# A two-layer decoder on one core: expert output products turned to features, the recurrence reordered, unread matmuls added

## The reference, cut to what matters

```python
# layer 0 experts: top 2 of 8, and a shared expert
y   = einsum('eth,ehd->etd', silu(xf @ w1[e]) * (xf @ w3[e]), w2[e])
out = einsum('etd,te->td', y, cw) + (silu(xf @ sw1) * (xf @ sw3)) @ sw2
# layer 1 recurrence
xi, z = split(x @ Win.T); lam = exp(-8 * softplus(omega) * sigmoid(xi @ Wl.T + bl)); v = xi @ Wv.T + bv
h = lam_t * (h - 2 * v_t * (v_t.h / v_t.v_t)) + (1 - lam_t) * xi_t     # over t, from h = xi_0
out = (silu(z) * h) @ Wout.T
# layer 1 experts
y = selu(x @ exp_wi[e] + bi) @ exp_wo[e] + bo, weighted by the top 2 of 8 of a gate network
```

## Time and profile before

| | us |
|---|---|
| median of 3 runs | 1028.47 |
| lowest, highest | 1027.62, 1028.54 |
| the profiled execution | 1027.66 |
| its span, first to last instruction | 1025.9 |
| PE busy | 890.1 (87%) |
| PE weight loads busy | 659.5 (64%) |
| DVE busy | 807.4 (79%) |
| ACT busy | 544.1 (53%) |
| POOL busy | 421.4 (41%) |

### The profile page before, as it was taken

The page is one execution under the profiler, slowest core; times in us unless marked ns, Lnnn a source line. Parts: engine busy times, 40 slices in busy tenths (PEclk is TensorE's granted clock), DMA queues, the critical chain, the costliest instruction groups (busy, mean ns, idle before and its releaser), DMA issues.

```text
span 1025.9 us, 15128 instructions
## 1 busy us (share of the span) xinstructions
PE 890.1 (87%) x5606; PEld 659.5 (64%) x5606; DVE 807.4 (79%) x1443; ACT 544.1 (53%) x980; POOL 421.4 (41%) x401
## 2 busy tenths in 40 slices
PE   5967777777989999998985875899999899999997
PEld 4422323232769888885653554576667799899997
DVE  6699999999776555563888787679997788788886
ACT  6456565655553222235652221556658757667774
POOL 6479999999310010110885244544431111011110
PEclk9979999999999999998986998879999999999999
DMA  6000000000000100100000000100000000000001
GB/s 189 1 0 1 0 1 1 0 1 1 1 1 17 32 16 16 32 1 0 1 1 0 1 1 1 41 2 3 2 2 2 1 22 21 22 1 22 26 16 42
DMA packets 19859, 13.80 MB, mean 13 GB/s; under 512 B 3067, under 2 KB 18313, under 8 KB 19786
## 3 DMA queue, kind: packets, MB, share of 16 engines
q1 hardware_dynamic: 19786, 12.84, 4.5%
HBM read 11.79 MB, written 1.05 MB: 13 GB/s over the span
## 4 chain that ended last, share of the span: by engine, by line
PE 55%; DVE 16%; ACT 5%; issue 4%; POOL 2%; DVEq 0%; ACTq 0%; POOLq 0%
PE ps L1416 19%; PE ps L1409 18%; PE ps L1629 3%; PE ps L1460 2%; PE ps L1749 2%; DVE small L1259 2%; POOL R L370 2%; DVE G L1262 1%; PE ps L1739 1%; PE ps L1699 1%; DVE R L1220 1%; DVE stats L838 1%; DVE ps L1225 1%; PE ps L1816 1%; DVE ps L1209 1%
## 5 line engine op out<-in xcount | busy, mean ns | idle before, releaser
L1416 PE MATMUL ps<-xhl,whl 128*128 128x512 f32 x960 | 245.8, 405 | 6.6 <-ACT G L655 1.9
L1416 PEld LDWEIGHTS ps<-xhl,whl 128*128 128x128 f32 x960 | 177.7, 192 | 45.2 <-issue 7.7
L1409 PEld LDWEIGHTS ps<-R,G 128*128 128x128 f32 x1024 | 120.6, 194 | 7.0 <-DVE G L1303 4.8
L1409 PE MATMUL ps<-R,G 128*128 128x128 f32 x1024 | 121.3, 277 | 4.1 <-DVE G L1303 4.1
L793 ACT ACTIVATE G<-ps,w_exp_bi 128x512 f32<-128x512 f32 x128 | 89.9, 702 | 63.5 <-PE ps L1416 52.5
L361 POOL TENSOR_TENSOR R<-G,R 128x1024 f32<-128x1024 f32 x43 | 100.5, 2353 | 19.7 <-ACT R L556 17.1
L655 ACT ACTIVATE G<-ps 128x512 f32<-128x512 f32 x72 | 42.8, 597 | 114.4 <-PE ps L1416 114.4
L968 DVE TENSOR_TENSOR_SCAN R<-ps,R 128x1024 f32<-128x1024 f32 x43 | 97.5, 2277 | 5.7 <-POOL R L370 5.7
L794 ACT ACTIVATE G<-ps,ebs 128x512 f32<-128x512 f32 x144 | 102.0, 708 | 0.0
L1065 DVE SCALAR_TENSOR_TENSOR X<-ps,cw,X 128x128 f32<-128x128 f32 x272 | 76.5, 343 | 23.4 <-PE ps L1409 23.2
L1439 PE MATMUL ps<-bc,sel 96*128 96x512 bf16 x128 | 46.4, 390 | 50.2 <-ACT LN L563 22.2
(11 more groups left out here) (276 smaller groups left out, 1721.0 us busy)
## 6 DMA issues: line engine op xcount, KB each, us to landing
ew<-in_w_dram SPq DMA_DIRECT2D x24, 128.0 KB, 2.2
R<-in_exp_wi_dram SPq DMA_DIRECT2D x8, 256.0 KB, 2.8
R<-in_exp_wo_dram SPq DMA_DIRECT2D x8, 256.0 KB, 3.2
X<-in_x_dram SPq DMA_DIRECT2D x4, 256.0 KB, 4.1
out_dram<-X SPq DMA_DIRECT2D x4, 256.0 KB, 2.3
w_ctxT<-in_ctxT_dram SPq DMA_DIRECT2D x1, 487.5 KB
ew<-in_sw_dram SPq DMA_DIRECT2D x3, 128.0 KB, 2.6
w_W_in<-in_W_in_dram SPq DMA_DIRECT2D x1, 256.0 KB, 3.1
```

The lines of the kernel that those rows point to most:

```text
L1409: ins = mm(bank(o)[:, 0, b * width:(b + 1) * width], lhs(k, b), rhs(k), start=k == 0, stop=k == ks - 1)
L1416: ins = mm(mix(out) if n == N_WIN1 else out, whl[:, wslot(n), i, m * P:(m + 1) * P], rhs, start=k == 0, stop=k == 2)
```

## The change: what it does

Most of the diff renames semaphores. What is left:

1. First experts: chunks 0 to 3 (shared expert) and 8 to 31 (experts 1 to 6) make their output product with the weights as the stationary operand, both operands split, 6 matmuls of 512 columns; the result has features on partitions. ACT copies the hidden chunk to an upper part, DVE subtracts for the lower one, GpSimd splits the output weights. The router's weights are turned by PE, written to DRAM by SP and read back spread over all partitions, one expert at a time. DVE multiplies and adds into `YT`; at the end PE turns it and DVE adds it to X. Chunks 4 to 7 and 32 to 35 stay as they were.
2. Recurrence: values before decays; sigmoid becomes tanh, 0.5 (1 + tanh(x/2)), with its constants in `coef`; xz(1) to xz(3) stand in group 0 after the spread; chunk_dots(g - 1) stand ahead of v_dot_v(g); squares are summed into 64 columns instead of one.
3. `unread(o, n)`: n fp32 matmuls of 128 columns, identity times identity, into a bank that nobody reads, at the places shown.
4. Second experts: selu of chunk 1 ahead of the ranking, of chunk 2 in it; output banks 4 to 7 for the first four chunks.

```diff
+            def hidden_upper(i):                                   # ACT
+                if i >= 2:
+                    act.wait_ge(S["down0"], i - 1)
+                for m in range(M0):
+                    act.wait_ge(S["hid0"], M0 * i + m + 1)
+                    sc.copy(hl[:, i % 2, 0, m * GT:(m + 1) * GT], hidr[:, i % 2, m * GT:(m + 1) * GT])
...
+            def hidden_lower(i):                                   # DVE
+                for m in range(M0):
+                    dve.wait_ge(S["hid_hi"], M0 * nth(i) + m + 1)
+                    v.tensor_tensor(hl[:, i % 2, 1, ...], hidr[:, i % 2, ...], hl[:, i % 2, 0, ...], ALU.subtract)
+            def weigh_out(c):
+                e, g = divmod(c, NG)
+                dve.wait_ge(S["down0"], c + 1)
+                dve.wait_ge(S["cw_odd" if e % 2 else "cw_even"], 16 * (e // 2))
+                v.tensor_tensor(yt_new[:, c % 2], bank(4 + c % 2)[:, 0, :], cwb[:, e % 2, gcols(g)], ALU.mult)
+            def add_out_T(c):
+                v.tensor_tensor(YT[:, gcols(g)], YT[:, gcols(g)], yt_new[:, c % 2], ALU.add)
...
             for i in range((E + 1) * NG + 1):
+                if i - 2 in by_feature[NG:]:
+                    weigh_out(i - 2)
                 if i < (E + 1) * NG:
-                    hidden(i)
+                    hidden(i, (lambda: add_out_T(i - 2)) if i - 2 in by_feature[NG:] else (lambda: None))
+                if i in by_feature:
+                    hidden_lower(i)
...
+                if k == 2:                                         # SP
+                    sp.wait_ge(S["cw_rows"], 1)
+                    sp.dma_start(cw_dram.rearrange("e (b t) -> b e t", t=T), cw_rows)
+                    sp.wait_ge(S["cw_rows"], 17)
+                if k and k * NG in by_feature:
+                    sp.dma_start(cwb[:, k % 2, :], cw_dram[k - 1].partition_broadcast(P))
...
+            def down_T(c):                                         # PE
+                for k in range(M0):
+                    pe.wait_ge(S["hid_lo"], M0 * n + k + 1)
+                    for p, (i, j) in enumerate(PARTS):
+                        ins = mm(bank(4 + c % 2)[:, 0, :], w2hl[:, e % 2, i, k * D:(k + 1) * D],
+                                 hl[:, c % 2, j, k * GT:(k + 1) * GT], start=k == p == 0, stop=k == M0 - 1 and p == 2)
...
-            for g in range(NG - 1):
-                transpose_xn(3, g)
+            transpose_xn(3, 0)
+            transpose_xn(3, 1)
+            pe.wait_ge(S["yt_res"], NG)
+            unread(7, 5)
+            transpose_xn(3, 2, between=3)
+            unread(7, 7)
...
             xz(0)
             transpose_xn(3, NG - 1)
-            xz(1)
             for g in range(NG):
                 pe.wait_ge(S["xz_ev"], 4 * g + HI)
-                lam_or_v(g, w["Wl"], (0, 1), "l_mm", (("v2_ev", HI * g), ("l_ev", HI * g)))
-                lam_or_v(g, w["Wv"], (2, 0), "v2_mm", (("v2_ev", HI * g - 1), ("l_ev", HI * g + 1)))
-                if g + 2 < NG:
-                    xz(g + 2)
+                lam_or_v(g, w["Wv"], (0, 1), "v2_mm", (("l_ev", HI * g), ("v2_ev", HI * g)))
+                lam_or_v(g, w["Wl"], (2, 0), "l_mm", (("l_ev", HI * g - 1), ("v2_ev", HI * g + 1)))
+                if g:
+                    chunk_dots(g - 1)
                 v_dot_v(g)
                 spread_reciprocal(g)
-                if g:
-                    chunk_dots(g - 1)
+                if g == 0:
+                    xz(1)
+                    xz(2)
+                    xz(3)
             chunk_dots(NG - 1)
...
+            pe.wait_ge(S["u_done"], 3 * (NG - 1))                  # ahead of the chunk loop
+            pe.wait_ge(S["c_done"], 2 * (NG - 1))
+            pe.wait_ge(S["e_ev"], NG - 1)
+            unread(5, 14)
...
+            unread(5, 34)                                          # behind the chunk loop
...
+                if g + 1 < NG:                                     # behind the values of groups 0 to 2
+                    pe.wait_ge(S["ln_xnT"], 4 * NG + 1)
+                    unread(0, 6)
...
+            unread(7, 8)                                           # ahead of the head loop
...
             selu_sum(0, 0, "act1", "hid1")
             gate_logits(3)
+            selu_sum(1, 1, "act1", "hid1")
             step(gate_top(3))
...
-            selu_sum(1, 1, "act1", "hid1")
+            dve.wait_ge(S["down1"], 1)
+            selu_sum(2, 0, "act1", "hid1")
```

More of the change, by code:

```diff
@@ L45 @@
 EB = 8
+VW = 64
 def decoder_program(nc, a, out):
@@ L194, in decoder_program @@
         cwT = G[0:E, 5, 1, :].rearrange("p (b t) -> p b t", b=B)
+        by_feature = [*range(NG), *range(2 * NG, E * NG)]
+        nth = by_feature.index
+        cwb = G[:, 0, :, :]
+        yt_new = G[:, 2, 0, 0:2 * GT].rearrange("p (s n) -> p s n", s=2)
+        cw_rows = G[:, 2, 0, 2 * GT:2 * GT + T]
+        YT = G[:, 2, 1, :]
+        cw_dram = nc.dram_tensor("cw_by_expert", (E, N), F32).ap()
         xi, z1, lam, vv, nb, ww = (GBUF(i) for i in range(6))
@@ L342, in _ @@
                                       pattern=[[-1, 32], [0, P]], channel_multiplier=1))
-            gp.memset(cw0[:], 1.0)
             step(gp.memset(hmask[:], 1.0))
@@ L686, in _ @@
             copy_xnT(3, NG - 1)
-            xz_copy(1)
             for g in range(NG):
                 for m in range(HI):
-                    act.wait_ge(S["l_mm"], HI * g + m + 1)
-                    sc.activation(row(lam[:, m], g), mix(bank(m)[:, 0, :]), ACT.Sigmoid, bias=w["bl"][:, m:m + 1])\
-                        .then_inc(S["l_ev"], 1)
-                for m in range(HI):
                     act.wait_ge(S["v2_mm"], HI * g + m + 1)
-                    sc.activation(row(vv[:, m], g), mix(bank(2 - 2 * m)[:, 0, :]), ACT.Identity, bias=w["bv"][:, m:m + 1])\
+                    sc.activation(row(vv[:, m], g), mix(bank(m)[:, 0, :]), ACT.Identity, bias=w["bv"][:, m:m + 1])\
                         .then_inc(S["v2_ev"], 1)
@@ L701, in _ @@
                 for m in range(HI):
+                    act.wait_ge(S["l_mm"], HI * g + m + 1)
+                    sc.activation(row(lam[:, m], g), mix(bank(2 - 2 * m)[:, 0, :]), ACT.Tanh, bias=coef[:, 0, m:m + 1], scale=0.5)\
+                        .then_inc(S["l_ev"], 1)
+                for m in range(HI):
                     act.wait_ge(S["l_ev"], HI * g + m + 1)
-                    sc.activation(row(lam[:, m], g), row(lam[:, m], g), ACT.Exp, scale=coef[:, 2, m:m + 1])\
+                    sc.activation(row(lam[:, m], g), row(lam[:, m], g), ACT.Exp, bias=coef[:, 2, m:m + 1], scale=coef[:, 2, m:m + 1])\
                         .then_inc(S["lam_done"], 1)
-                if g + 2 < NG:
-                    xz_copy(g + 2)
+                if g == 0:
+                    xz_copy(1)
+                    xz_copy(2)
+                    xz_copy(3)
                 if g >= 1:
@@ L1396, in _, with unread, transpose_xn @@
             mm = nc.tensor.matmul
-            def transpose_xn(i, g):
+            def unread(o, n):
+                for _ in range(n):
+                    mm(bank(o)[:, 0, 0:P], ident[:], ident[:], start=True, stop=True)
+            def transpose_xn(i, g, between=0):
                 for b in range(GB):
+                    if b == GB // 2:
+                        unread(7, between)
                     if b % (GB // 2) == 0:
@@ L1419, in _ @@
             pe.wait_ge(S["const"], 1)
+            unread(7, 18)
             transpose_xn(0, 0)
+            unread(7, 5)
             for g in range(NG):
@@ L1424, in _ @@
                     transpose_xn(0, g + 1)
+                if g == 0:
+                    unread(7, 3)
                 pe.wait_ge(S["w_split"], 1)
@@ L1576, in router_logits, with transpose_YT @@
                 ins.then_inc(S["rt_mm"], 1)
+            def down_T(c):
+                e, n = c // NG, nth(c)
+                pe.wait_ge(S["w2_split"], n // NG + 1)
+                if c >= 2:
+                    pe.wait_ge(S["res0"], c - 1)
+                for k in range(M0):
[3 more added lines that the diff above has]
+                                 hl[:, c % 2, j, k * GT:(k + 1) * GT], start=k == p == 0, stop=k == M0 - 1 and p == 2)
+                ins.then_inc(S["down0"], 1)
+            def transpose_YT(g):
+                pe.wait_ge(S["yt_acc"], (E - 3) * NG + g + 1)
+                if g >= 2:
+                    pe.wait_ge(S["yt_res"], g - 1)
+                for b in range(GB):
+                    ins = nc.tensor.transpose(bank(6 + g % 2)[:, 0, b * D:(b + 1) * D], YT[:, (g * GB + b) * T:(g * GB + b + 1) * T], ident[:])
+                ins.then_inc(S["yt_mm"], 1)
             for i in range((E + 1) * NG + 1):
```

165 lines of the change are left out of this document (117 added, 48 removed).

## The result

The changed kernel ran in 1024.21 us (median of 20 runs, 1020.17 to 1033.13), the kernel before in 1028.88 beside it (20 runs, 1026.59 to 1035.64). The ratio is 0.9948, with a 95% interval from 0.9927 to 0.9969: 5.4 us faster by the ratio, 4.7 by the medians. 1025.3 was predicted, so the time came out close. The gain did not: 2.8 us were forecast, and the kernel before had a median 0.4 us higher here than in the runs that the forecast started from. The stages show that the total is a sum of opposite terms, some of which hang on TensorE's clock and differ from one execution to the next.

A forecast was written before the change was run, and what follows sets the result against it. PE was taken to bound both expert stages, DVE's work per group the recurrence, with DVE and PE alternating in chunk loop and heads. Terms -7.5 + 16 - 1.2 - 1.8 - 0.8 - 4 - 3.5 = -2.8 gave 1025.3 us, range 1017 to 1036.

The forecast's parts named there:

- First experts, -7.5 predicted: First experts: output product by features in 28 chunks gains 11.5 us, added costs leave -7.5 (-9 to 0).
- turned result: First experts: turning the result back takes 16 transposes, 4 x 0.58, +2.3 us.
- the tail: End of first experts: DVE has last feature chunks, additions of the turned result and norm together, +1.0 us.
- Rival 3: First experts: DVE becomes the bound, six instructions at 0.75, the -7.5 becomes 0, time 1033 us; chance 0.12.
- The sentence of the Trainium skill: First experts, DVE: next instruction waits until the pipe has emptied; about 1 us of gain would go, not in the sum.
- Recurrence, +16 predicted: Layer 1 recurrence: dots ahead of squares leave DVE waiting 8.2 us per group, twice; +16 us (+11.5 to +23).
- Rival 1: Recurrence, groups 2 and 3: whole exposed stretch runs at 1.2 GHz, 11.7 instead of 8.2 us each, 1032; chance 0.20.
- rival 2: Recurrence: clock survives the wait, 5.9 us exposed each; head loop gets its whole 5.4; time 1019; chance 0.24.
- Rival 4: Wherever unread matmuls were added: they don't keep the clock, 10.5 us lost, time 1036; chance 0.06.
- the start: Start of the program: unread matmuls change nothing, 0, since ACT reaches its first silu at 16.44 by its own queue.
- the heads: Head loop: 8 unread matmuls ahead of it bring back time lost to the low clock, -4 us (0 to -5.4).
- Second experts: Second experts: selu ahead of the ranking lets the second output product start 2.9 us earlier and warm, -3.5 (0 to -4.8).

The follow-up runs named there:

- experiment 5: Changed kernel without its unread matmuls, except the older two per step in the chunk loop: 1032.08 us, ratio 1.0006.
- 3: Changed kernel with the projections of layer 1 placed as before, dots still ahead of the squares: 1035.13 us, ratio 1.0047.
- 6: Changed kernel with four instead of six matmuls per chunk in the output product by features, which changes what is computed: 1035.49 us, one execution.
- experiment 7: Changed kernel with selu of chunks 1 and 2 of the second experts back behind the ranking, four output banks kept: 1026.0 us, one execution.
- experiment 1: Changed kernel with the dots of group g-1 back behind the spread of group g, early projections kept: 1011.13 us, ratio 0.98.
- 2: Changed kernel with both recurrence moves undone, dots behind the spread and projections as before: 1009.02 us, ratio 0.98.
- experiment 4: Changed kernel plus 36 unread matmuls behind the products of groups 2 and 3, while TensorE waits for the solve: 1024.66 us, ratio 0.9942.
- experiment 9: Kernel of experiment 1 with 17 instead of 8 unread matmuls ahead of the head loop: 1004.74 us, ratio 0.9777.

## Why the prediction was right, step by step

The mechanism of each large term held. That the time came out 1.1 us from the forecast is in part luck, since the misses of the stages have opposite signs; in the profiled execution, 1022.9 for 1024.9, it was 2.0.

**First experts, -7.5 predicted, -9.8 measured.** The working held: 4.08 us per chunk for 4.11, DVE's starts 0.60 apart, PE the bound. By steps: 24 chunks at 0.44 are -10.6 and the shared expert's four, which are less regular, -0.8 (together -11.5 predicted, -11.4 measured). The turned result cost 2.6 (2.3), the tail 0.3 instead of 1.0, and splits and first broadcast 0.2 instead of 0.7. The remaining -1.5 I had not foreseen: the input product of chunk 1 came at the full clock, 3.00 for 4.55. No part of the change is shown to have done that. It took 4.58 in experiment 5 without unread matmuls, but also in 3, 6 and 7 with them, and 3.00 in 1, 2 and 4; so the changed code's own part is nearer to -8.3. A third or more of the 1.5 is not even gained: in every kernel where this product took 3.0, the one of chunk 0 ahead of it took 3.51 to 4.11 for 3.00, which the first row of the table carries. Rival 3 was nearer than its 0.12 said: with some 0.04 us of slack per chunk, one more instruction on DVE, at 0.60, would by this have made DVE the bound.

The sentence of the Trainium skill that I had weighed (VectorE: DVE Perf Modes, The DRAIN you can't avoid) was only half of what the page says. Its next section, Two Vector instructions with no wait between them, names the case in which an instruction is held until the earlier ones have finished: its inputs or output start in another quadrant of partitions than those before it. All six here span the 128 partitions and are not held, and the trace agrees: 0.68 us long, started 0.59 to 0.61 apart.

**Recurrence, +16 predicted, +14.0 measured.** The mechanism was right at each point that could be read. The reciprocal of group 1 was put at t0 + 34.4 and came at 34.2. Groups 2 and 3 were to wait 6 to 10 us for the squares, 8.2 by the sum, and waited 7.96 and 7.69. The dots took 5.9 and 5.7 us (6.5 predicted, 4.16 at full clock), the squares 1.74. Of the 2.0 us too many, 0.8 is this exposure, 0.6 DVE's own work per group (16.4 and 16.5 for 16.8 and 16.7), 0.4 the last group and 0.2 the way to group 1. Rival 1 (all cold) did not come, since the clock was back before the squares; rival 2 (all warm) is what experiment 4 built, and it is worth 3.3 in the stage. That the early projections are not to blame is shown by experiments 1 and 2.

**Unread matmuls.** Rival 4 is refuted as a whole: without them the kernel is 6.0 us slower by the ratios, 7.9 by the medians and 9.2 in the profile, for 10.5 predicted. Chunk loop steps are 1.97 from the first on, and the output product of layer 1 took 7.38 us for 9.47. The one step that failed is the start, put at 0 and measured at +1.9. I argued that ACT's first silu decides at 16.44 whatever happens ahead of it. The silu came at 16.67, yet the second projection, with PE idle for 2.60 us ahead of it, ran at 4.49 us for 2.98. The matmuls had warmed the first projection, which nobody needed earlier, and so left a longer wait ahead of the second, 2.60 us for 1.38. It was cold in six of the eight kernels with this start and warm in the two without unread matmuls (2.98, 3.01). But the longer wait doesn't settle it: in two of the eight it ran warm behind the same wait. The changed kernel's, then that of experiment 9:

```profile
17.42 4.49 PE L1516 MATMUL ps<-xhl,whl 128*128 128x512 f32 x12 [2.60 <-ACT G L582]
```
```profile
17.68 3.01 PE L1516 MATMUL ps<-xhl,whl 128*128 128x512 f32 x12 [2.61 <-ACT G L582]
```

Nor is it the whole +1.9. Experiment 5 had the warm second projection and no unread matmuls, and came to the product of chunk 1 at 297.38, where the changed kernel came at 297.94 and the one before at 296.02. The eight kernels with this start lie between 294.77 and 297.94. So what the 0 left out is a start whose length differs by some 3 us between executions: 1.5 are the second projection, cold or warm, and 2.2 the VectorE multiply named in experiment 1. What these matmuls themselves cost there is open.

For the heads I had -4, and -3.1 came in an execution that kept its clock. One that loses it is worse than no matmuls at all: 107.91 us where the kernel before took 103.71 and experiment 5 took 103.95. Over the seven profiled executions with 8 matmuls the mean is 103.9, so over these seven the matmuls brought nothing; that the changed kernel's profiled execution got its -3.1 is luck too.

**Second experts.** -3.5 against -3.4, and experiment 7 returns exactly this.

So the time was 1.1 us off while single stages were off by up to 2.3, in both directions: +1.9 at the start and +0.9 in the heads against -2.3 in the first experts, -2.0 in the recurrence and -0.5 between loop and heads. And the largest thing in the diff was avoidable: without the dots ahead of the squares the rest of the change is worth 2.0% instead of 0.5%.

## What to carry to other kernels

When two engines alternate, look at what the second one does while the first works, and keep it on the far side of the wait. Here one line moved across two others made each engine wait 8 us for the other, twice. Before an engine is given more work because it "is idle more than half of the time", measure its own cadence by cutting the other engine's work: the averages hid that one chunk in four was slow. Unread matmuls that end 2 to 3 us before the work they are for left the clock uncertain here: behind such a wait it held in some executions and not in others, and the time that was lost when it fell was more than the time that was gained when it held. A wide spread between runs of one kernel was the hint to look there. One trace per kernel is too little to price such a term; compare several kernels that share the code.

## What the runs showed of the hardware

- After waits of the same 1.98 to 1.99 us, with the same instructions around them, the granted clock stayed at 1.00 in the changed kernel's execution and went to 0.50 for 8 us in experiment 4's. The price in the head loop was 7.3 us. The Trainium skill (TensorE: Matmul & The Clock Gate, What's actually happening) calls the number of slow matmuls at a kernel's start variable from run to run; here the same is seen in mid-kernel. It puts the cost below 1% of a typical kernel; the executions of experiment 1's kernel lay 0.9% apart.
- The clock fell while TensorE was never idle: over the router's 32 matmuls and what follows them it read 0.67 (304 to 312 us, experiment 9, TensorE busy in all of the 8.00 us), and the product behind them took 2.91 us for 1.6.
- Behind waits of 8.4 to 8.5 us the first twelve matmuls took 4.3 to 5.5 us for 2.8. The four after these took 1.46 to 1.62 us for 1.46, and the sixteen squares behind them their usual 1.89.
- DVE instructions with all operands in SBUF went from 0.68 to as much as 1.80 us beside GpSimd's splits, with or without DMA at the same time, while those that read PSUM stayed at 0.67 to 0.69.
